# Two cross attentions on one core: a slot's four score matmuls issued before the row-maximum matmuls

## The reference

```python
# layer 0: 16 heads of 32
qn, kn, vn = layer_norm(x), layer_norm(ctx), layer_norm(ctx)
Q, K, V = qn @ wq + bq, kn @ wk + bk, vn @ wv + bv
attn = softmax(Q K^T / sqrt(32)); x = x + (attn V) @ wo + bo
x = x + gelu(layer_norm(x) @ w1 + b1) @ w2 + b2
# layer 1: 16 heads of 64
attn = softmax((x Wq / 8) (ctx Wk)^T - 0.5); out = (attn (ctx Wv)) @ Wfc + x
return layer_norm(out)
```

## Time and profile before

| What | Value |
|---|---|
| Runs | 1605.43, 1613.99, 1622.47 us |
| Span of the profiled execution | 1604.4 us |
| Time of the profiled execution | not listed by itself; the shortest run is 1.0 us above the span |
| Attention 0, slots with projection and scores | about 127 to 536 us |
| Attention 0, the last steps | about 536 to 575 us |
| Attention 1 | about 857 to 1540 us |
| TensorE busy over the span | 1418.0 us (88%) |
| VectorE busy | 935.5 us (58%) |
| ScalarE busy | 666.4 us (42%) |
| GpSimd busy | 431.3 us (27%) |

### The profile page before, as it was taken

How to read it: one execution, slowest core, us unless ns; L and a number is a source line. 1 busy time by engine, 2 the same in 40 slices (tenths; PEclk the granted TensorE clock), 3 DMA queues, 4 the chain that set the end, 5 groups by cost and what they waited for, 6 DMA issues and landing times. The chain is left out here.

```text
span 1604.4 us, 34148 instructions
## 1 busy us (share of the span) xinstructions
PE 1418.0 (88%) x12908; PEld 900.5 (56%) x12908; DVE 935.5 (58%) x1677; ACT 666.4 (42%) x1294; POOL 431.3 (27%) x487
## 2 busy tenths in 40 slices
PE   5497898899999756999959999999999999999968
PEld 3255566566656532544435666666666666666653
DVE  5856788798887747622343555454544454555444
ACT  1324565566555534421122444444444444444441
POOL 3212444455443445020000111111111111111124
PEclk9798999999999766999979999999999999999979
DMA  4263333323332033210284333334333333332221
GB/s 139 64 175 103 107 74 103 109 69 107 105 104 64 28 95 112 72 60 27 75 241 105 101 95 75 90 101 102 101 95 84 98 95 81 101 101 65 57 84 65
DMA packets 117005, 149.59 MB, mean 93 GB/s; under 512 B 51056, under 2 KB 92528, under 8 KB 113776
## 3 DMA queue, kind: packets, MB, share of 16 engines
q1 hardware_dynamic: 116848, 147.34, 33.5%
HBM read 71.12 MB, written 22.48 MB: 58 GB/s over the span
## 5 line engine op out<-in xcount | busy, mean ns | idle before, releaser
L642 POOL TENSOR_TENSOR attn_probs<-attn_p,attn_probs 128x400 f16<-128x400 f32 x192 | 188.1, 980 | 915.1 <-ACT attn_probs L993 914.9
L1112 DVE TENSOR_REDUCE attn_nmax<-attn_p_max 100x1 f32<-100x722 f32 x256 | 231.3, 904 | 109.2 <-PE attn_p_max L839 102.8
L817 PE MATMUL attn_p_proj<-attn_ctxT,kv_w_k 128*128 128x361 f16 x1536 | 251.6, 319 | 21.7 <-DMA attn_ctxT<-ctxT_parts 18.2
L822 PE MATMUL attn_p_proj<-kv_w_v,attn_ctxT 128*128 128x512 f16 (+1 forms) x1152 | 264.3, 379 | 0.0
L983 ACT ACTIVATE attn_p<-attn_p_sc,attn_score_bias 128x400 f32<-128x400 f32 x192 | 113.5, 591 | 299.4 <-PE attn_p_sc L868 298.6
L817 PEld LDWEIGHTS attn_p_proj<-attn_ctxT,kv_w_k 128*128 128x128 f16 x1536 | 145.4, 98 | 107.9 <-DMA attn_ctxT<-ctxT_parts 18.6
L993 ACT CAST attn_probs<-attn_p 128x400 f16<-128x400 f32 (+1 forms) x384 | 197.8, 516 | 0.0
L822 PEld LDWEIGHTS attn_p_proj<-kv_w_v,attn_ctxT 128*128 128x128 f16 (+1 forms) x1152 | 110.4, 101 | 111.0
L642 DVE TENSOR_TENSOR attn_probs<-attn_p,attn_probs 128x400 f16<-128x400 f32 (+1 forms) x192 | 119.9, 625 | 89.2 <-ACT attn_probs L993 88.5
L983 ACT ACTIVATE attn_p<-attn_p_sc 128x400 f32<-128x400 f32 x192 | 95.8, 499 | 152.4 <-PE attn_p_sc L864 150.0
L822 PE MATMUL attn_p_proj<-l_w_v,attn_ctxT 128*128 128x512 f16 (+1 forms) x576 | 136.2, 388 | 0.8 <-DVE attn_vbuf L1159 0.8
(11 more groups left out here) (179 smaller groups left out, 2570.6 us busy)
## 6 DMA issues: line engine op xcount, KB each, us to landing
attn_ctxT<-ctxT_parts SPq DMA_DIRECT2D x16, 1444.0 KB, 6.5
attn_kstack_a<-attn_knat SPq DMA_DIRECT2D x128, 180.5 KB, 3.5
attn_kstack<-attn_knat SPq DMA_DIRECT2D x192, 90.2 KB, 2.2
ctxT_parts<-attn_ctxT SPq DMA_DIRECT2D x8, 1444.0 KB, 5.9
attn_kstack_b<-attn_knat SPq DMA_DIRECT2D x64, 180.5 KB, 3.6
attn_c<-in_ctx_dram SPq DMA_DIRECT2D x40, 256.0 KB, 3.2
rows_wo_w<-in_L_xattn_w_dram SPq DMA_DIRECT2D x8, 512.0 KB, 3.6
cols_w_w<-in_L_xattn_w_dram SPq DMA_DIRECT2D x4, 1024.0 KB, 5.5
```

Source lines behind the costliest of these rows:

```text
L642: eng.tensor_tensor(probs[:r, g % 2, 1, t, :HG * SQ], p32[:r, t % 3, :], probs[:r, g % 2, 0, t, :HG * SQ], ALU.subtract).then_inc(p_lo_mad ...
L817: last = pe.matmul(bank[:, :HALF], w_k[:, wa, k, c0 + m * P:c0 + (m + 1) * P], ctxT[:, par, ca, k, n * HALF:(n + 1) * HALF], **flags)
L822: last = pe.matmul(bank[:r, :], ctxT[:, par, ca, k, P * t:P * t + r], w_v[:, wa, k, c0:c0 + E], **flags)
L1112: dve.tensor_reduce(nmax[:SQ, hh:hh + 1], p_max[:SQ, :, :HALF], AX.XY, ALU.max, negate=True).then_inc(max_made, 1)
```

## The change

In TensorE's `step`, the call of `scores` moves ahead of the two calls of `max_scores` (only one of which is made in a slot). The arguments, the waits inside each call and all other engines' code stay as they are. It applies to both attentions.

```diff
                 for j in range(sl.n):
                     g, t = divmod(j, KT)
+                    if has_scores:
+                        scores(s, s - 1, 1 - par, g, t)
                     if g < NG - 1 and has_scores and t < HG:
                         max_scores(s - 1, 1 - par, g + 1, t)
                     if g == NG - 1 and proj and t < HG:
                         max_scores(s, par, 0, t)
-                    if has_scores:
-                        scores(s, s - 1, 1 - par, g, t)
                     if prep and j in sl.ctx:
                         ctx_transposes(s, par, sl.ctx[j])
```

## The result

The changed kernel took 1627.86 us in the median of 7 runs (1627.53 to 1633.94), the kernel before 1615.38 us in 7 runs: a ratio of 1.0082 with an interval of 1.0053 to 1.0111. The profiled execution of the changed kernel took 1633.94 us, with a span of 1631.8.

A forecast was written before the change was run, and what follows sets the result against it. TensorE was taken to bound attention 1, and attention 0 with VectorE close behind. The terms −5.3 + 5.6 − 1.3 − 1.0 gave −2.0 us from the 1613.99 us median: 1612 us, range 1599 to 1625 us.

The forecast's parts named there:

- How a stall answers: TensorE's stream: a stall loses, wins or keeps time by which call its chain leaves TensorE and at which it returns.
- The two kinds that return at a maximum: Chain from maximum to next maximum: no change; chain from elsewhere to a maximum: one score group won per stall.
- Attention 1, slot 1: Second projection's wait for VectorE's evacuation: scores 0.31 us sooner win 17 × 0.31 = 5.3 us; bounds 6.3 won and 0.
- Attention 1, slots 2 and 3: Slots with two projections: 0, as VectorE's waits for ScalarE, 0.50 and 0.55 us, exceed its reduction's 0.37 us delay.
- second projections that wait in slots 2 and 3: Attention 1: a sign named beforehand that would show the forecast wrong.
- Attention 1, slot 10: Maximum's transpose waits for VectorE's reduction, split and output copy: each stall grows 0.37 us, 15 × 0.37 = 5.6 us lost.
- Attention 0, slot 20: Long stalls before a maximum: the score group fits inside, seven × 0.19 = 1.3 us won; bounds −2.6 and +1.3.
- the last steps: Both attentions, slots without projections: earlier scores shorten VectorE's wait for ScalarE's probabilities, −1.0 us; bounds −2 and +0.7.
- The slower one: Attention 1, slots 1 to 3: VectorE's late reduction delays every second projection, +16.7 us; 1642 us in all; chance 0.06.
- the granted clock of the window in attention 0: Sign against the forecast if it leaves 0.96 by over 0.01; the clock rival claimed −7.5 us, 1604.5 us, chance 0.12.
- ScalarE's lead: Attention 0: if all 32 VectorE waits for probabilities were on the path, 9.9 us more won, 1602 us; chance 0.06.
- The rule of the Trainium skill: Attention 0: starting the reduction later is wrong way round for TensorE's gaps, 30 × 0.19 = +5.7 us; part of the slower rival.

## Why the prediction was wrong, step by step

- **How a stall answers** held where it could be measured: the loss at slot 10 was 0.37 us where nothing collided, and the stall of slot 1 went. The two kinds that return at a maximum are only in attention 0, and its −2.8 us don't tell them apart.
- **Attention 1, slot 1: −5.3 us.** Right by itself: its waits vanished, and attention 1 was 6.1 us shorter where nothing else was in the way. But in the changed kernel the same kind of loss, 0.35 us (1076.32 − 1074.13 from start to start, less 1.84), came back in slot 3, where L1119 was held up and made VectorE's evacuation late for the second projection (15 waits, 3.2 us).
- **Attention 1, slots 2 and 3: 0.** This is a step that failed. I set the 0.37 us delay against VectorE's wait of 0.55 us for ScalarE and took the split's length as fixed. It grew by up to 0.70 us, and 15 × 0.35 = 5.3 us were lost where I had put 0. The sign that the prediction named for this, second projections that wait in slots 2 and 3, came.
- **Attention 1, slot 10: +5.6 us, bounds 0 and 5.6.** The term that was mis-sized. It measured 15 × 1.07 = 16 us, 0.37 of each from the later reduction and 0.70 from the held-up split. The upper bound was wrong as well: it bounded the delay of the reduction but not what VectorE's next operations would meet at their new time.
- **The sum for attention 1.** −6.1 + 16 + 5.3 = +15.2 us against 17.3 in the profile; some 2 us are not accounted for.
- **Attention 0, slot 20, and the last steps: −2.3 us together.** The kernel with that change alone measured −2.8 us, with an interval from −5.7 to +0.2: agreement, no proof. The stall itself can't be read at 0.2 us: in the unit where it was 2.46 us long before and 3.52 in the changed kernel, it was 3.67 in the kernel that keeps the old order in attention 0.
- **The rivals.** The slower one named the right engine and one of the right slots, slot 3, but another mechanism, and gave it 0.06. One sign that I had named did come: the granted clock of the window in attention 0 fell from 0.96 to 0.93. It didn't decide, for it was 0.95 in the kernel that keeps the old order there and 0.94 in the one that has the new order there alone, and the latter was not slower. ScalarE's lead did not decide either. The rule of the Trainium skill (Perfetto Trace Analysis, "Optimization Strategy") to make what ends a gap start sooner I had set aside for attention 0; slot 10 of attention 1 is a gap of TensorE too, and there the reduction that ends it started 0.37 us later and the gap grew by 1.07.
- **What I overlooked** was a co-runner. The moved score group makes ScalarE and then GpSimd sooner, the moved maximum makes VectorE later; I followed each alone and never laid GpSimd's row beside VectorE's, though both were 0.6 us apart in the trace. Nor did I see that the kernel before has such collisions already, in attention 0: 5 of its 32 L1119 and 6 of its 32 L1121 took over 0.3 us, each to within 0.03 us of the end of a GpSimd operation. One of them, VectorE and GpSimd:

```profile
289.75 1.07 DVE L1121 SCALAR_TENSOR_TENSOR attn_nmax_parts<-attn_nmax,attn_nmax_parts 100x4 f16<-100x4 f32 x1
```

```profile
289.65 1.16 POOL L1279 TENSOR_TENSOR attn_cparts<-attn_c,attn_cparts 128x512 f16<-128x512 f32 x1
```

The kernel before scatters (1605 to 1624 us over the comparisons). Its first three runs had a median of 1613.99, the later groups 1615 to 1617; this took about 2 us off the forecast.

## What to carry to other kernels

When an order is changed, list what every engine will be doing at the new times, and not only who waits for whom: here a shift of 0.68 us between VectorE and GpSimd became a wait of 0.70 us, most of GpSimd's 0.94. Keep an operation that sits on a critical chain clear of the other engine's large ones, by order or by a form that isn't held up (here the one-source reduction). And look at a tiny operation whose duration equals what is left of another engine's: its length is a wait, and the profile counts it as busy time.

## What the runs showed that was not expected

- A VectorE operation of four columns took 0.87 us beside a GpSimd operation of 0.94 us, and 0.17 us otherwise; it ended within 0.02 us of GpSimd's end.
- On SBUF operands, a one-source reduction (157 ns) was not held up; a scalar addition (0.87 us against 0.17) and an operation with two SBUF sources (0.62 us against 0.16) were.
- The kernel before scatters from 1605 to 1624 us, while six of the seven runs of the changed kernel lie between 1627.53 and 1628.21. The kernel with the new order in attention 1 alone scatters again, from 1625.07 to 1632.97. Why is open.
